# A decoder's cross-attention: written-out pipeline of five blocks, half-block PSUM, 32-row scores, squares and inner norm on ScalarE

## The reference

```
Qp = query @ Wq + bq;  K = l2norm(key @ Wk + bk);  V = value @ Wv + bv
Q = l2norm(Qp)                          # over the whole row of 256
attn = softmax(Q K^T * 0.25) per head;  out = (attn V) @ Wo + bo
r = layernorm(out + Qp) * gamma + beta  # the inner norm
x = layernorm(x + r)                    # the outer norm
```

## Time and profile before

| | us |
|---|---|
| median of 3 runs (3962.21 to 3969.09) | 3966.22 |
| the profiled execution | 3963.41 |
| its span, first to last instruction | 3961.7 |
| PE busy in the span | 3342.7 (84%) |
| DVE busy | 2966.7 (75%) |
| ACT busy | 2018.7 (51%) |
| POOL busy | 834.5 (21%) |

### The profile page before, as it was taken

The page is one execution under the profiler, slowest core; times in us unless marked ns, Lnnn a source line. Parts: engine busy times, 40 slices in busy tenths (PEclk is TensorE's granted clock), DMA queues, the critical chain, the costliest instruction groups (busy, mean ns, idle before and its releaser), DMA issues. The chain is left out here.

```text
span 3961.7 us, 63658 instructions
## 1 busy us (share of the span) xinstructions
PE 3342.7 (84%) x23832; PEld 1675.0 (42%) x23832; DVE 2966.7 (75%) x5058; ACT 2018.7 (51%) x3821; POOL 834.5 (21%) x1135
## 2 busy tenths in 40 slices
PE   8499998576399859999999999999857689998758
PEld 4244444443277523333333333333334345554625
DVE  7688885556477779999999999999364367776375
ACT  3167766133133217888888888888712223334120
POOL 4232333123233420000000000000114344445000
PEclk9599999798699969999999999999877789999678
DMA  4322220100000320000000000000002221100202
GB/s 171 106 54 50 50 50 21 38 22 6 22 1 1 115 91 26 18 18 26 18 18 26 18 18 26 18 18 18 4 8 74 106 78 35 45 23 3 91 14 80
DMA packets 78693, 161.27 MB, mean 41 GB/s; under 512 B 21464, under 2 KB 38880, under 8 KB 78272
## 3 DMA queue, kind: packets, MB, share of 16 engines
q1 hardware_dynamic: 74176, 153.17, 13.0%
q10 hardware_dynamic: 4224, 4.19, 0.3%
HBM read 87.76 MB, written 54.72 MB: 36 GB/s over the span
## 5 line engine op out<-in xcount | busy, mean ns | idle before, releaser
L582 ACT ACTIVATE L_attn_E<-L_attn_psS 128x512 f32<-128x512 f32 (+3 forms) x2816 | 1448.9, 569 | 374.4 <-PE L_attn_psS L724 339.2
L656 DVE TENSOR_REDUCE L_attn_tops<-L_attn_psM 128x2 f32<-128x1024 f32 x1152 | 1395.9, 1223 | 94.3 <-PE L_attn_psM L774 83.5
L774 PE MATMUL L_attn_psM<-L_attn_K,L_attn_Q 62*128 62x512 f32 (+3 forms) x2816 | 982.6, 457 | 103.4 <-DMA L_attn_K<-parts_k 72.2
L724 PE MATMUL L_attn_psS<-L_attn_Q,L_attn_K 64*128 64x512 f32 (+3 forms) x2816 | 1018.2, 439 | 41.3 <-DMA L_attn_Q<-L_attn_mparts 36.4
L745 PE MATMUL L_attn_psO<-L_attn_E,L_attn_V 128*32 128x256 f32 (+1 forms) x10752 | 850.1, 388 | 21.6 <-ACT L_attn_oT L592 21.0
L724 PEld LDWEIGHTS L_attn_psS<-L_attn_Q,L_attn_K 64*128 64x128 f32 x2816 | 438.8, 187 | 576.6 <-ACT L_attn_E L582 479.8
L774 PEld LDWEIGHTS L_attn_psM<-L_attn_K,L_attn_Q 62*128 62x128 f32 x2816 | 410.9, 192 | 156.3 <-issue 74.7
L745 PEld LDWEIGHTS L_attn_psO<-L_attn_E,L_attn_V 128*32 128x32 f32 x10752 | 212.7, 108 | 475.9 <-issue 265.7
L538 POOL TENSOR_TENSOR L_AO<-L_attn_o 128x128 f32<-128x128 f32 x64 | 29.3, 458 | 1375.0 <-DVE L_attn_o L689 1375.0
L650 DVE CUSTOM_DVE_ANT_0 L_attn_psM<-L_attn_psM,L_attn_wide 128x128 f32<-128x128 f32 (+3 forms) x512 | 240.4, 514 | 52.2 <-PE L_attn_psM L774 49.2
L2225 ACT ACTIVATE x_E<-x_psS 128x512 f32<-128x512 f32 x256 | 138.9, 595 | 176.5 <-PE x_psS L2348 164.3
(11 more groups left out here) (347 smaller groups left out, 3870.0 us busy)
## 6 DMA issues: line engine op xcount, KB each, us to landing
parts_q<-L_proj_parts SPq DMA_DIRECT2D x64, 256.0 KB
parts_k<-L_proj_parts SPq DMA_DIRECT2D x64, 256.0 KB
L_attn_Q<-parts_q SPq DMA_DIRECT2D x192, 64.0 KB
L_attn_K<-parts_k SPq DMA_DIRECT2D x192, 64.0 KB
L_attn_Q<-parts_q SPq DMA_DIRECT2D x64, 128.0 KB
L_attn_K<-parts_k SPq DMA_DIRECT2D x64, 128.0 KB
queries<-x1p_qo SPq DMA_DIRECT2D x16, 512.0 KB
keys<-x1p_ko SPq DMA_DIRECT2D x16, 512.0 KB
```

The source lines that it names most:

```text
L582: act.activation(E[(4 * n + s) % (4 * RING)][:, c0:], psS[bank][:, c0:], ACT.Exp, scale=scale).then_inc(e_done, 1)
L656: dve.tensor_reduce(dst, src, AX, ALU.max).then_inc(m_read, 1)
L724: pe.matmul(psS[bank][:, c0:], K[g.slot][r:r + RH, c, kt * P:(kt + 1) * P], Q[g.slot][r:r + RH, c, q * HALF + c0:(q + 1) * HALF], start=Tr ...
L774: last = pe.matmul(psM[bank][:, j * HALF:j * HALF + n], Q[t.slot][r:r + TOP, c, qt * P:(qt + 1) * P], K[t.slot][r:r + TOP, c, h * HALF:h * ...
```

## The change

The turns are written out, twelve of them, each with up to five blocks alive (t, u = t-1, v = t-2, x = t-3, o = t-4). PSUM is held in halves of a block, one bank each: psT for X transposes and output products, psQ for projections and query transposes, psS for scores, psO for values and psZ for sums. Scores use 32 rows of KB and of qT per pair of heads, so KB is built once for all batch entries (with parity, two columns, for heads8). Values are read from VBD in place. ACT squares the queries with a running sum and does the inner norm as Identity with a scale and a bias (nm = -mean times inverse deviation, from DVE); POOL scales the queries to unit length. Most tiles are doubled (qb, for QP, is threefold). wq and wo are loaded in the setup, X is read in place of xs. Within a turn, PE splits scores into four pairs and values into two halves, and so do ACT and DVE.

The core of the diff, moved left for width. Waits that only keep a doubled tile from being overwritten too early are left out, and so are the old functions, which the listing above shows.

```diff
-                     (heads8[:], a["heads8"])):
+                     (parity[:], a["parity"])):
         sp.dma_start(dst, src).then_inc(loaded, 16)
+    for dst, src in ((keep["x0_wq"], "L0x_wq"), (keep["x0_wo"], "L0x_wo")):
+        sp.dma_start(dst[:], a[src]).then_inc(keep["x0_weights"], 16)
...
-        psA = m.ps("x0_psA", BLK * D)
+        psT = [m.ps(f"x0_psT{k}", HALF) for k in range(2)]
+        psQ = [m.ps(f"x0_psQ{k}", HALF) for k in range(2)]
         psS = [m.ps(f"x0_psS{k}", HALF) for k in range(2)]
-        psO = [m.ps(f"x0_psO{k}", HALF) for k in range(2)]
+        psO, psZ = m.ps("x0_psO", HALF), m.ps("x0_psZ", HALF)
...
+    def turn_x(t):
+        for h in range(2):
...
             for c in range(DC):
+                for k in range(2):
+                    last = pe.transpose(psT[h][:, (2 * c + k) * P:(2 * c + k + 1) * P],
+                                        X[:, tile(t, 2 * h + k), c * P:(c + 1) * P], ident[:])
+            last.then_inc(x_turned, 1)
+    def queries(t):
+        for h in range(2):
+            pe.wait_ge(xT_in, 2 * t + h + 1)
...
+            for k in range(2):
                 for c in range(DC):
+                    last = pe.matmul(psQ[h][:, k * D:(k + 1) * D], xT[t % 2][:, c, (2 * h + k) * P:(2 * h + k + 1) * P],
+                                     wq[:, c, :], start=(c == 0), stop=(c == DC - 1))
+            last.then_inc(q_made, 1)
...
+    def scores(u, pair):
+        if u == 0 and pair == 0:
+            pe.wait_ge(kb_in, 2)
+        pe.wait_ge(qT_in, 2 * u + 2)
+        for hp in (2 * pair, 2 * pair + 1):
+            c, rows = hp // 4, slice(32 * (hp % 4), 32 * (hp % 4) + 32)
+            if 8 * u + hp >= 2:
+                pe.wait_ge(e_done, 8 * u + hp - 1)
+            pe.matmul(psS[hp % 2][:], KB[rows, c * B + u // PER, :, :].rearrange("p h k -> p (h k)"),
+                      qT[u % 2][rows, c, :], start=True, stop=True).then_inc(s_done, 1)
+    def values(u, c):
+        pe.wait_ge(e_done, 8 * u + 4 * c + 4)
+        if u or c:
+            pe.wait_ge(divided, 4 * u + 2 * c)
+        for out, lhs in ((psZ, None), (psO, VBD)):
+            for j in range(4):
+                last = pe.matmul(out[32 * j:32 * j + 32, :], OB[:] if lhs is None else lhs[:, u // PER, 4 * c + j, :],
+                                 E[:, 4 * c + j, :], start=True, stop=True)
+            last.then_inc(o_made, 1)
+    def product(v):
+        pe.wait_ge(divided, 4 * v + 4)
+        for h in range(2):
...
+            pe.wait_ge(xT_in, min(2 * (v + 2) + h + 1, 2 * NB))
+            for k in range(2):
                 for c in range(DC):
+                    last = pe.matmul(psT[h][:, k * D:(k + 1) * D], aT[v % 2][:, c, (2 * h + k) * P:(2 * h + k + 1) * P],
+                                     wo[:, c, :], start=(c == 0), stop=(c == DC - 1))
+            last.then_inc(c_made, 1)
+    def turn(t, u, v, *_):
+        if t is not None:
+            turn_x(t)
+        if u is not None:
+            scores(u, 0)
+        if t is not None:
+            queries(t)
+        if u is not None:
+            scores(u, 1)
+            values(u, 0)
+        if v is not None:
+            product(v)
+        if u is not None:
+            scores(u, 2)
+            scores(u, 3)
+        if t is not None:
+            turn_q(t)
+        if u is not None:
+            values(u, 1)
...
+    def copy(ps, to, made, done, u):
+        for h in range(2):
+            act.wait_ge(made, 2 * u + h + 1)
+            act.activation(to[u % 2][:, :, h * D:(h + 1) * D], ps[h][:].rearrange("p (c n) -> p c n", c=DC),
+                           ACT.Copy).then_inc(done, 1)
+    def exps(u, pair):
+        if pair % 2 == 0 and u >= 1:
+            act.wait_ge(o_made, 4 * (u - 1) + pair + 2)
+        for hp in (2 * pair, 2 * pair + 1):
+            act.wait_ge(s_done, 8 * u + hp + 1)
+            act.activation(E[:, hp, :], psS[hp % 2][:], ACT.Exp, scale=0.25).then_inc(e_done, 1)
+    def square(t):
...
+        for k in range(BLK):
+            act.wait_ge(qp_in, 2 * t + k // 2 + 1)
...
+            act.activation(sq[:], qp[t % 2][:, k, :], ACT.Square, accum_out=ss[t % 2][:, k:k + 1]).then_inc(squared, 1)
...
+    def deviation(n, u, summed, rooted_, freed):
+        act.wait_ge(summed, 2 * u + 2)
...
+        act.activation(sd[n][u % 2][:], mv[n][u % 2][:, :, 1], ACT.Sqrt, bias=eps[:]).then_inc(rooted_, 1)
+    def normal(x):
+        act.wait_ge(inner_mul, 2 * x + 2)
...
+        for k in range(BLK):
+            last = act.activation(z[x % 2][:, k, :], y[x % 2][:, k, :], ACT.Identity, bias=nm[x % 2][:, k:k + 1],
+                                  scale=rs[0][x % 2][:, k:k + 1])
+        last.then_inc(z_in, 1)
+    def turn(t, u, v, x, o):
+        if t is not None:
+            copy(psT, xT, x_turned, xT_in, t)
+        if u is not None:
+            exps(u, 0)
+            exps(u, 1)
+        if t is not None:
+            square(t)
+            root(t)
+        if x is not None:
+            deviation(0, x, inner_sum, inner_root, inner_mul)
+        if o is not None:
+            deviation(1, o, outer_sum, outer_root, outer_norm)
+        if x is not None:
+            normal(x)
+        if u is not None:
+            exps(u, 2)
+            exps(u, 3)
+        if t is not None:
+            copy(psQ, qT, q_turned, qT_in, t)
+    turns(turn)
...
+    for h in range(2):
+        pool.tensor_tensor(KB[:, :, h, :], KT[:].rearrange("p c b k -> p (c b) k"),
+                           parity[:, h:h + 1].unsqueeze(2).broadcast_to([P, DC * B, 64]), ALU.mult).then_inc(kb_in, 1)
+    def biased(t):
+        pool.wait_ge(qp_in, 2 * t + 2)
...
+        pool.tensor_tensor(qb[t % 3][:], qp[t % 2][:], bo[:].unsqueeze(1).broadcast_to([P, BLK, D]), ALU.add).then_inc(qb_in, 1)
+    def unit(t):
+        pool.wait_ge(rn_in, 2 * t + 2)
+        for h in range(2):
...
+            k = slice(2 * h, 2 * h + 2)
+            pool.tensor_tensor(qn[t % 2][:, k, :], qp[t % 2][:, k, :],
+                               rn[t % 2][:, k].unsqueeze(2).broadcast_to([P, 2, D]), ALU.mult).then_inc(qn_in, 1)
+    def residual(x):
+        s = x % 2
+        pool.wait_ge(z_in, x + 1)
...
+        pool.wait_ge(z_pool, 3 * x + 2)
...
+        pool.tensor_tensor(w[s][:], zb[s][:], X[:, tile(x, 0):tile(x + 1, 0), :], ALU.add).then_inc(z_pool, 1)
+    def turn(t, u, v, x, o):
+        if t is not None:
+            biased(t)
+            unit(t)
+        if x is not None:
+            residual(x)
+    turns(turn)
...
+    def projected(t):
+        for h in range(2):
+            dve.wait_ge(q_made, 2 * t + h + 1)
...
+            dve.tensor_tensor(qp[t % 2][:, 2 * h:2 * h + 2, :], psQ[h][:].rearrange("p (k d) -> p k d", k=2),
+                              bq[:].unsqueeze(1).broadcast_to([P, 2, D]), ALU.add).then_inc(qp_in, 1)
+    def length(t):
+        s = t % 2
+        dve.wait_ge(rooted, t + 1)
+        dve.tensor_scalar(ns[s][:], nr[s][:], 1e-12, None, ALU.max).then_inc(rn_in, 1)
+        dve.wait_ge(rn_in, 2 * t + 1)
...
+        dve.reciprocal(rn[s][:], ns[s][:]).then_inc(rn_in, 1)
+    def divide(u, c):
+        dve.wait_ge(o_made, 4 * u + 2 * c + 1)
+        dve.reciprocal(rec[c][:], psZ[:]).then_inc(divided, 1)
+        dve.wait_ge(divided, 4 * u + 2 * c + 1)
+        dve.wait_ge(o_made, 4 * u + 2 * c + 2)
...
+        dve.tensor_tensor(aT[u % 2][:, c, :], psO[:], rec[c][:], ALU.mult).then_inc(divided, 1)
+    def add(v):
+        for h in range(2):
+            dve.wait_ge(c_made, 2 * v + h + 1)
+            dve.wait_ge(qb_in, v + 1)
...
+            dve.tensor_tensor(y[v % 2][:, 2 * h:2 * h + 2, :], psT[h][:].rearrange("p (k d) -> p k d", k=2),
+                              qb[v % 3][:, 2 * h:2 * h + 2, :], ALU.add).then_inc(y_in, 1)
+    def sums(n, u, src, summed, rooted_):
+        s = u % 2
         for k in range(BLK):
+            last = dve.bn_stats(st[n][s][:, k, :], src[s][:, k, :])
+        last.then_inc(summed, 1)
+        dve.wait_ge(summed, 2 * u + 1)
...
         for k in range(BLK):
+            last = dve.bn_aggr(mv[n][s][:, k, :], st[n][s][:, k, :])
+        last.then_inc(summed, 1)
+    def inner_scale(x):
+        s = x % 2
+        dve.wait_ge(inner_root, x + 1)
...
+        dve.reciprocal(rs[0][s][:], sd[0][s][:]).then_inc(inner_mul, 1)
+        dve.wait_ge(inner_mul, 2 * x + 1)
+        dve.scalar_tensor_tensor(nm[s][:], in0=mv[0][s][:, :, 0], scalar=-1.0, in1=rs[0][s][:], op0=ALU.mult,
+                                 op1=ALU.mult).then_inc(inner_mul, 1)
+    def outer(o):
+        s = o % 2
+        dve.wait_ge(outer_root, o + 1)
+        dve.reciprocal(rs[1][s][:], sd[1][s][:]).then_inc(outer_norm, 1)
+        dve.wait_ge(outer_norm, 2 * o + 1)
         for k in range(BLK):
+            last = dve.tensor_scalar(X[:, tile(o, k), :], w[s][:, k, :], mv[1][s][:, k, 0:1], rs[1][s][:, k:k + 1],
+                                     ALU.subtract, ALU.mult)
+        last.then_inc(outer_norm, 1)
+    def turn(t, u, v, x, o):
```

(35 more changed lines are left out.)

276 lines of the change are left out of this document (83 added, 193 removed).

## The result

The changed kernel took 3906.32 us (median of 4 runs, 3903.36 to 3916.87) beside 3967.65 us for the kernel before (4 runs, 3962.21 to 3974.95) on the same chip. The ratio is 0.9844, with a 95% interval of 0.9821 to 0.9866: faster by 61 us (1.6%), where I had forecast 107 and a range that ended at 3882. A second measurement, of five runs, gave 3892.11 us and a ratio of 0.9805 (0.9780 to 0.9829).

What follows compares the result with a forecast made beforehand. One chain through all engines set the 34 us turn. Turns of 14.1 + 21.0 + 19.2 + 104.0 and a drain of 47.2 summed to 205.5 against 312.35, 106.8 less: 3859 us, range 3845 to 3882.

Steps and rivals of the forecast that it cites:

- The 4.7 us of the start: Stage start: wq and wo load under the setup and X is read in place, taking 4.7 us off.
- third load: ScalarE: two table loads a turn were forecast; a third would be a sign that the forecast was wrong.
- Half clock: Rival: PE's idle 2.3 us before S3 drops its clock, 3.5 us lost in six turns: 3880; chance 0.17.
- S3: PE's fourth pair of score products in a turn, forecast after about 2.3 us of PE idle time.
- TQ: PE's query transposes behind S3: forecast before the last exp, needing the unit queries at 18.2 us.
- V1: PE's second half of the values, last in the turn: forecast to start at 19.0 and take 1.8 us.
- then inverts and scales the mean for the inner norm (0.4): 12.7.: DVE's small operations after the root, ahead of ScalarE's inner norms: 0.4 us, done 12.7 us into the turn.
- All hidden: POOL's 13 us a turn and the other work beside the chain were claimed to add nothing to the turn.
- P ends at 13.4 and exp 4 starts at 14.4 instead of 16.0: Turn 2, without inner norm: output product ends at 13.4, first exp of S2 starts at 14.4; turn 19.2 us.
- S2: PE's third pair of score products, behind the output product; forecast to wait in PSUM for its exps.
- V0: PE's first half of the values, ahead of the output product: forecast from 7.9 to 9.8 us.
- Drain (turns 8 to 11), DVE- and then POOL-bound: Last turns of the stage, summed along VectorE and then GpSimd: 47.2 us, second division over at 19.7.

Runs made afterwards that it cites:

- the fill: Changed kernel plus six unused 128x128 by 256 products per turn, placed on PE ahead of S3: ratio 0.9767 to the kernel before, stage 218.3 us.
- five fillers: Changed kernel plus five unused products per turn ahead of S3, and VectorE's inner scale ahead of the lengths: ratio 0.9762, stage 214.6 us.
- after: The changed kernel itself, as profiled, against the kernel before: 3906.32 us, ratio 0.9844; measured again 0.9805, stage 234.3 us.
- scale first: Changed kernel with VectorE scaling the mean for the inner norm before it clamps and inverts the lengths: ratio 0.9783, stage 231.8 us.

## Why the prediction was wrong

The direction and the mechanism were right: the stage became a pipeline with a turn of about 24 instead of 34 us, and the saving comes from there. The size was wrong: 78.0 us instead of 106.8. The missing 28.8 are -1.3 (turn 0), 16.7 (clock, turns 1 to 7), 7.8 (the rest of turns 1 to 7) and 5.6 (drain).

**What held.** The 4.7 us of the start: from the setup's first transfer to the stage it is 29.17 us before and 29.23 after, and the second number now ends at a product. The pair of score products in different row groups runs together. Squares at 0.58 each (forecast 0.60), inner norms at 2.07 for four (2.0). No third load. The Trainium skill (ScalarE: Activation LUTs, What ACT_TABLE_LOAD costs) has a drain at each switch; the load at 877.77 starts 0.01 us after the last square and the root 0.02 after its end, so by this trace too there is none. GpSimd is busy 11.45 us a turn (forecast 13).

**"Half clock"**, the rival to which I gave 0.17, is what happened. The step that failed is the assumption under S3, TQ and V1 that an idle time of 2.3 us costs nothing but itself. It was 2.75 us, S3, TQ and V1 then ran at half speed (V1 in part), and the fill took back 16.7 us over seven turns (24.99 - 21.75 and so on). My price for it, 3.5 us in six turns, was 21. Two neighbours were on record, 1.1 us (no fall) and 8.83 (a fall); I took the near end for the likelier.

**"then inverts and scales the mean for the inner norm (0.4): 12.7."** It ended 13.24 us into the turn, since L1447 took 1.04 us beside GpSimd. Price 0.63 us a turn (21.73 to 21.10), 3 us in five turns. The Trainium skill (SBUF — State Buffer, SBUF: two separate sides) says that VectorE and GpSimd share a pair of ports, which one of them holds for a whole instruction, when VectorE has two inputs in SBUF or runs in a mode that uses both ports. The rows agree for L1447, which has two inputs in SBUF: it took as long as one of the two 1.02 us passes that had started beside it. The outer norm, with one large input, took 7.66 us until the third pass was over; which of the two conditions holds for it no run shows. I had asked what hides GpSimd's work ("All hidden") and not what it does to its neighbour.

**"P ends at 13.4 and exp 4 starts at 14.4 instead of 16.0"** (turn 2). S2 was over at about 14.7 and the load, which the sum left out, comes behind it in ScalarE's queue: 16.0. With the clock at 1.00 turn 2 took 21.10 us with five fillers, 1.9 over the forecast, and with S2 ahead of V0 18.73, under the forecast. In the full turns the norms hid the same wait.

**"Drain (turns 8 to 11), DVE- and then POOL-bound"**, with the second division over at 19.7. I summed VectorE alone. In turn 8 of after:

```profile
970.90 4.45 PE L1249 MATMUL x_psT<-x_wo,x_aT 128*128 128x256 f32 x16
...
975.28 1.13 PE L1228 MATMUL x_psS<-x_qT,x_KB 32*128 32x512 f32 x4
...
976.48 1.28 ACT L1290 ACT_TABLE_LOAD   x1 [5.08 <-PE x_psS L1228]
...
981.39 1.93 PE L1237 MATMUL x_psZ<-x_E,L0x_OB 128*32 128x512 f32 x8 [0.69 <-ACT x_E L1290]
```

S2 waits behind the output product, which runs partly at half clock, the load behind S2, the exps behind the load and V1 behind the exps: the second division ends at 24.8 us of the drain instead of 19.7, and what follows takes 28.0 us where 27.5 were forecast. In "scale first", where V0 and the output product of this turn ran at full clock, it ends at 22.3: 2.5 of the 5.1 us are the clock here. The rest I read from the order of the queues; no run isolates it.

**The range.** It reached to the half clock alone, 3880. But the cases were not exclusive: the half clock and 12 us of small waits came together, which gives 3888 on the median, close to what the second measurement's ratio gives (0.9805 x 3966.22 = 3888.9). The first measurement lay another 16 us higher.

## What to carry to other kernels

Where a sum leaves the matrix engine with a gap of a few us a turn, price the products behind the gap at both clock levels before the gap counts as free, and try a filler. When an engine's queue is reordered, list for each waiting instruction what stands ahead of it in both queues that feed it: here exp 4 was held twice, and each edit alone gained nothing or little in the full turns. When two variants are compared by one profile each, look first at the turns in which they have the same instructions: turn 1 alone differed by 3.1 us here. Put a two-input or two-pointer operation of VectorE where GpSimd is idle, or give it to ScalarE.
